# Three cross-attentions with the last key's shares turned beside the inverse sums, and two changes of order in other sublayers

## The reference

```
L1/L2/L3 cross-attention (16 heads of 16 features; 257 keys):
  q = ln(x) Wq + bq;  k = ctx Wk + bk;  v = ctx Wv + bv
  w = softmax(q.k * scale + bias or mask)        # over 257 keys
  x += (w v) Wo + bo
L1 attention (complex, one head): two real parts of q.k summed, softmax over 32 keys, x += out Wo + bo
L0 feed-forward: layer norm twice; 8 fixed experts, 256 rows each:
  xa = ln2 A + b + ln1;  h = gelu(xa W1[e] + b1[e]);  o = h W2[e] + b2[e];  x += gelu(o N + bn)
```

## Time and profile before

| | before |
|---|---|
| median of 3 runs | 3566.3 us (3560.57 to 3572.57) |
| profiled execution | 3571.8 us, its span 3570.0 us |
| mean granted TensorE clock | 0.958 of full |
| busy PE / its weight loads | 3298.9 us (92%) / 2646.9 us (74%) |
| busy DVE / ACT / POOL | 2152.4 (60%) / 1428.5 (40%) / 1017.6 (29%) us |

### The profile page before, as it was taken

How to read it: one execution, slowest core, us unless ns; L and a number is a source line. 1 busy time by engine, 2 the same in 40 slices (tenths; PEclk the granted TensorE clock), 3 DMA queues, 4 the chain that set the end, 5 groups by cost and what they waited for, 6 DMA issues and landing times. The chain is left out here.

```text
span 3570.0 us, 105629 instructions
## 1 busy us (share of the span) xinstructions
PE 3298.9 (92%) x39322; PEld 2646.9 (74%) x39322; DVE 2152.4 (60%) x7124; ACT 1428.5 (40%) x4209; POOL 1017.6 (29%) x1587
## 2 busy tenths in 40 slices
PE   8988889999986999999999999887999999998799
PEld 6767777777765888888877777774666788878576
DVE  3766225555656888889645555763334566558545
ACT  2334335555532333333245555541111455555222
POOL 0112113333342444445333333442110111112421
PEclk9999999999997999999999999978999999999799
DMA  6653334212103000000041111033112411110323
GB/s 208 216 175 154 102 94 108 61 56 56 64 1 140 3 3 3 2 3 2 2 99 43 40 47 46 2 111 124 46 47 72 87 38 38 41 34 2 108 79 114
DMA packets 149258, 238.26 MB, mean 67 GB/s; under 512 B 14456, under 2 KB 121720, under 8 KB 147176
## 3 DMA queue, kind: packets, MB, share of 16 engines
q1 hardware_dynamic: 138816, 203.16, 18.2%
q0 software_dynamic: 10176, 31.47, 3.1%
HBM read 213.61 MB, written 38.94 MB: 71 GB/s over the span
## 5 line engine op out<-in xcount | busy, mean ns | idle before, releaser
L3299 POOL TENSOR_TENSOR l1fu_second_weighed<-l1fu_second,l1fu_parts 128x256 bf16<-128x256 bf16 x384 | 278.7, 753 | 339.2 <-DVE l1fu_second L3540 332.3
L3351 PEld LDWEIGHTS l1fu_ps_u<-l1f_xnT_all,l1f_key_in 128*128 128x128 f32 x2048 | 252.0, 195 | 17.3 <-issue 11.0
L3351 PE MATMUL l1fu_ps_u<-l1f_xnT_all,l1f_key_in 128*128 (+1 forms) x2048 | 254.9, 278 | 8.6 <-issue 5.5
L3362 PE MATMUL l1fu_ps_y<-l1f_key_out,l1fu_units 128*128 128x256 f32 x1024 | 250.6, 389 | 2.0 <-DVE l1fu_units L3548 2.0
L3362 PEld LDWEIGHTS l1fu_ps_y<-l1f_key_out,l1fu_units 128*128 128x128 f32 x1024 | 185.7, 190 | 33.6 <-issue 6.2
L3413 ACT COPY l1fu_plane<-l1fu_ps_p 128x512 f32<-128x512 f32 x128 | 75.1, 586 | 250.4 <-PE l1fu_ps_p L3341 250.4
L3535 DVE TENSOR_TENSOR l1fu_first<-l1fu_index,l1fu_counted 128x1024 bf16<-128x1024 bf16 x128 | 166.8, 1303 | 12.8 <-PE l1fu_ps_p L3341 9.6
L3421 ACT ACTIVATE l1fu_units<-l1fu_ps_u 128x512 f32<-128x512 f32 x128 | 76.6, 598 | 151.9 <-PE l1fu_ps_y L3362 139.9
L1020 ACT ACTIVATE l3x_scores<-l3x_scores,l3x_minus_big 128x257 f32<-128x257 f32 x256 | 129.0, 511 | 2.3 <-DVE l3x_minus_big L1109 2.3
L1020 ACT ACTIVATE l1x_scores<-l1x_scores,l1x_minus_big 128x257 f32<-128x257 f32 x256 | 128.9, 511 | 2.1 <-DVE l1x_minus_big L1109 2.1
L1020 ACT ACTIVATE l2x_scores<-l2x_scores,l2x_minus_big 128x257 f32<-128x257 f32 x256 | 128.8, 511 | 2.1 <-DVE l2x_minus_big L1109 2.1
(11 more groups left out here) (743 smaller groups left out, 8383.6 us busy)
## 6 DMA issues: line engine op xcount, KB each, us to landing
rows_by_expert<-in_zeros_dram SPq DMA_DIRECT2D x1, 17544.0 KB
l0x_ctxT<-in_ctx_T_dram SPq DMA_DIRECT2D x32, 514.0 KB, 5.2
l0x_ctx_rows<-in_ctx_dram SPq DMA_DIRECT2D x64, 256.0 KB, 3.3
l0f_w<-in_L_ffn_w_dram SPq DMA_DIRECT2D x16, 1024.0 KB, 5.2
l1x_ctx_sb<-in_ctx_T_dram SPq DMA_DIRECT2D x64, 256.0 KB, 2.8
l2x_ctx_sb<-in_ctx_T_dram SPq DMA_DIRECT2D x64, 256.0 KB, 2.8
l3x_ctx_sb<-in_ctx_T_dram SPq DMA_DIRECT2D x64, 256.0 KB, 2.8
l1x_mask_raw<-in_mask_int_dram SPq DMA_DIRECT2D x16, 514.0 KB, 3.9
```

Source lines behind the costliest of these rows:

```text
L3299: last = nc.gpsimd.tensor_tensor(second_weighed[:, k % 2, part], second[:, k % 2], parts[:, 1 - par, part, TC * k:TC * k + TC].unsqueeze(2 ...
L3351: last = nc.tensor.matmul(ps_u[:, k % 2, j, :], key_in[:, c, JS * k + j, :], xnT_all[:, c, bass.ts(tile, P)], start=(c == 0), stop=(c == C ...
L3362: last = nc.tensor.matmul(ps_y, units[:, k, j, :], key_out[:, JS * k + j, :], start=(k + j == 0), stop=(k == K - 1 and j == JS - 1))
```

## The change

In cross-attention the last key's share no longer holds its values. POOL spreads the bare probability (`tail_share`) with the table that `share` uses; PE turns it beside `share` into the other half of `ps_share`; ACT copies both in one copy of 256 columns; DVE multiplies it with the last key's values, now kept by feature (`v_last`, a number for each partition), adds the output from PSUM, in two instructions of 64 columns, and then weighs from SBUF. The matmul against the identity is gone. The trip through device memory is gone; instead POOL copies `v_last` once a tile. In complex attention `next_norm` stands after `turn_probs`. In the fixed experts the turning of half 1 stands between the two output halves of the second layer, and ACT keeps it before the expert's output.

```diff
@@ cross_attention: gpsimd
+            def put_tail_values(i, n):
+                after(pool, per_batch["o_with_last"][BT - 1], n - 1)
+                nc.gpsimd.tensor_copy(v_last[:], v_tail[:, :, bass.ds(i * BT, BT)]).then_inc(s["tail_values_put"], 1)
...
-            def shares(i, at, before2):
+            def shares(at, before2):
                 if before2:
-                    pool.wait_ge(per_batch["o_ready"][before2[0]], before2[1])
+                    pool.wait_ge(per_batch["shares_turned"][before2[0]], before2[1])
                 pool.wait_ge(per_batch["exp_ready"][b], n)
                 nc.gpsimd.tensor_tensor(tail_share[:, b % 2], scores[:, b, :, K2].unsqueeze(2).broadcast_to([P, R, 32]),
-                                        tails[:, i, b].rearrange("p (r d) -> p r d", r=R), ALU.mult).then_inc(
-                    per_batch["tail_share_ready"][b], 1)
+                                        core.table("same_half").unsqueeze(1).broadcast_to([P, R, 32]),
+                                        ALU.mult).then_inc(per_batch["tail_share_ready"][b], 1)
...
+                    if not first and t == 0:
+                        put_tail_values(i, n)
                     if ahead:
-                        if first and t == BT - 1:
-                            pool.wait_ge(s["rest_of_tails"], 32)
-                        shares(i + (t + 1) // BT, ahead, before)
+                        shares(ahead, before)
-            def load_tails(name, first, count):
...
@@ tensor
-                for c in range(C):
-                    last = nc.tensor.matmul(ps_vt, ctx_tail[:, c, :], wt["v"][:, c, :],
-                                            start=(c == 0), stop=(c == C - 1))
+                for oc in range(C):
+                    for c in range(C):
+                        last = nc.tensor.matmul(ps_vt[:, oc * B:oc * B + B], wt["v"][:, c, oc * P:oc * P + P],
+                                                ctx_tail[:, c, :], start=(c == 0),
+                                                stop=(c == C - 1 and "bv" not in rows))
+                    if "bv" in rows:
+                        last = nc.tensor.matmul(ps_vt[:, oc * B:oc * B + B], rows["bv"][0:1, oc * P:oc * P + P],
+                                                core.table("ones", 1)[:, 0:B], start=False, stop=True)
...
             def turn_shares(at, before):
                 if before:
-                    pe.wait_ge(per_batch["o_weighed"][before[0]], before[1])
+                    pe.wait_ge(per_batch["o_with_last"][before[0]], before[1])
+                pe.wait_ge(per_batch["tail_share_ready"][b], n)
+                nc.tensor.transpose(ps_share[:, P:2 * P], tail_share[:, b % 2].rearrange("p r d -> p (r d)"), ident)
                 pe.wait_ge(per_batch["share_ready"][b], n)
-                nc.tensor.transpose(ps_share, share[:, b % 2].rearrange("p r d -> p (r d)"), ident).then_inc(
+                nc.tensor.transpose(ps_share[:, 0:P], share[:, b % 2].rearrange("p r d -> p (r d)"), ident).then_inc(
                     per_batch["shares_turned"][b], 1)
...
             def outputs(at):
                 pe.wait_ge(per_batch["shares_kept"][b], n)
-                pe.wait_ge(per_batch["tail_share_ready"][b], n)
-                nc.tensor.matmul(ps_out, tail_share[:, b % 2].rearrange("p r d -> p (r d)"), ident, start=True,
-                                 stop=False, skip_group_check=True)
...
@@ scalar
-                nc.scalar.copy(shareT[:, b % 2], ps_share).then_inc(per_batch["shares_kept"][b], 1)
+                nc.scalar.copy(shareT[:, b % 2].rearrange("p a n -> p (a n)"), ps_share).then_inc(
+                    per_batch["shares_kept"][b], 1)
@@ vector
+                dve.wait_ge(s["tail_values_put"], n)
                 dve.wait_ge(per_batch["o_ready"][b], n)
-                nc.vector.tensor_tensor(weighed[:].rearrange("p c h q -> p (c h q)"), ps_out, shareT[:, b % 2],
+                for c in range(C):
+                    of_chunk = slice(64 * c, 64 * c + 64)
+                    last = nc.vector.scalar_tensor_tensor(lastT[:, of_chunk], shareT[:, b % 2, 1, of_chunk],
+                                                          v_last[:, c, b:b + 1], ps_out[:, of_chunk], ALU.mult,
+                                                          ALU.add)
+                last.then_inc(per_batch["o_with_last"][b], 1)
+                dve.wait_ge(per_batch["o_with_last"][b], n)
+                nc.vector.tensor_tensor(weighed[:].rearrange("p c h q -> p (c h q)"), lastT[:], shareT[:, b % 2, 0],
                                         ALU.mult).then_inc(per_batch["o_weighed"][b], 1)
@@ complex_attention: vector turn
-                if there(i, -1):
-                    next_norm(i - 1, i)
                 if there(i, 3):
                     norm_stats(dve, nc, s, i + 4, core.x[:, i + 3, :], stats[:], mean[:])
                 if there(i, 0):
                     turn_probs(i + 1)
+                if there(i, -1):
+                    next_norm(i - 1, i)
@@ fixed_experts_ffn: tensor turn
                 if now:
-                    second_layer(e + 1)
+                    second_layer(e + 1, 0)
                 if ahead:
                     turn_normed(e + 2, 1)
+                if now:
+                    second_layer(e + 1, 1)
+                if ahead:
                     projection(e + 2)
@@ fixed_experts_ffn: scalar turn
                     keep_turned(e + 2, 0)
+                    keep_turned(e + 2, 1)
                 if now:
                     keep_expert_output(e + 1)
-                if ahead:
-                    keep_turned(e + 2, 1)
-                if now:
```

More of the change, by code:

```diff
@@ L647, in cross_attention @@
                      exp_ready inv_ready share_ready tail_share_ready probs_turned_1 probs_turned_2 probsT_1 probsT_2
-                     shares_turned shares_kept o_ready o_weighed oT_kept""".split()}
+                     shares_turned shares_kept o_ready o_with_last o_weighed oT_kept""".split()}
         pack = core.pack(tag)
@@ L658, in cross_attention @@
         k_tail = sb("k_tail", [P, C, B])
-        v_tail = sb("v_tail", [B, D])
-        tails = sb("tails", [P, NT, BT, P])
+        v_tail, v_last = sb("v_tail", [P, C, B]), sb("v_last", [P, C, BT])
         kT = sb("kT", [P, BT, C, KEYS])
@@ L677, in cross_attention @@
         ps_o, ps_x = ps("ps_o", [P, 512]), ps("ps_x", [P, 512])
-        ps_out, ps_share, ps_kt = ps_o[:, 0:P], ps_o[:, P:2 * P], ps_o[:, 256:256 + C * B]
+        ps_out, ps_share = ps_o[:, 0:P], ps_o[:, P:3 * P]
+        ps_kt, ps_vt = ps_o[:, 256:256 + C * B], ps_p[:].rearrange("p r k -> p (r k)")[:, 0:C * B]
         ps_q, ps_y = ps_x[:, 0:D], ps_x[:, D:2 * D]
-        ps_vt = ps_p[0:B].rearrange("p r k -> p (r k)")[:, 0:D]
         def halves(bank):
@@ L798, in _ @@
             put_tail_keys(0, 1)
+            mask_bias(1)
             pool.wait_ge(s["tail_values"], 1)
-            nc.gpsimd.dma_start(core.tail_values, v_tail[:]).then_inc(s["tail_stored"], 16)
-            mask_bias(1)
-            pool.wait_ge(s["tail_stored"], 16)
-            load_tails("first_tails", 0, 1)
-            load_tails("rest_of_tails", 1, NT - 1)
-            pool.wait_ge(s["first_tails"], 32)
-            shares(0, (0, 1), None)
+            put_tail_values(0, 1)
+            shares((0, 1), None)
             all_tiles(pool, turn)
@@ L918, in outputs @@
                                 ps_out[of_pair, 64 * c:64 * c + 64], v[:, b, kc, c * P + 32 * r:c * P + 32 * r + 32],
-                                probsT[:, b % 2, kc, r, 64 * c:64 * c + 64], start=False, stop=(kc == 1),
+                                probsT[:, b % 2, kc, r, 64 * c:64 * c + 64], start=(kc == 0), stop=(kc == 1),
                                 skip_group_check=True, tile_position=(0, 32 * r))
@@ L1001, in keep_tail_keys, with keep_tail_values @@
                 last.then_inc(s["tail_keys"], 1)
+            def keep_tail_values():
+                act.wait_ge(s["tail_values_ready"], 1)
+                nc.scalar.copy(v_tail[:].rearrange("p c b -> p (c b)"), ps_vt).then_inc(s["tail_values"], 1)
             def keep_keys(at, src=ps_kv):
@@ L1058, in _ @@
             keep_tail_keys()
+            keep_tail_values()
             keep_keys((0, 1), first_keys[0])
@@ L1086, in spread_q @@
                 last.then_inc(s["q_spread"], 1)
-            def keep_tail_values():
-                dve.wait_ge(s["tail_values_ready"], 1)
-                if "bv" in rows:
-                    nc.vector.tensor_tensor(v_tail[:], ps_vt, rows["bv"][0:B], ALU.add).then_inc(s["tail_values"], 1)
-                else:
-                    nc.vector.tensor_copy(v_tail[:], ps_vt).then_inc(s["tail_values"], 1)
             def maxima(at):
@@ L2137, in first_layer, with second_layer @@
                     last.then_inc(h_ready[k], 1)
-            def second_layer(n):
-                pe.wait_ge(s["w2_loaded"], n * 32)
-                after(pe, s["eoT_ready"], n - 1)
```

(18 more changed lines are left out.)

10 lines of the change are left out of this document (2 added, 8 removed).

## The result

Median 3513.1 us (3511.7 to 3519.6, 4 runs) against 3563.4 us (3558.7 to 3572.6, 4 runs) of the kernel before on the same chip: ratio 0.9854, 95% interval 0.9836 to 0.9873, so 50.3 us less. The profiled execution took 3514.2 us, with a span of 3512.3 us; before's took 3571.8 us. The forecast was 3514 us. The total fits; one of its three terms, the cross-attentions, does not, as the tile periods show. The tile period is the distance of two tile outputs (L929 before, L925 after) on PE.

What follows compares the result with a forecast made beforehand. PE's stream bounds the cross-attentions, a DVE and POOL chain l1a, PE's stream with holes l0f. Savings of 30.8 + 7.0 + 15.2 = 53 us from the profiled 3571.8, adjusted to the median, gave 3514 us; 8-in-10 range 3500 to 3533.

Steps and rivals of the forecast that it cites:

- L909's removal, 0.32 us: Cross-attention, PE: without the identity matmul, L917 starts loading when L854's last stream ends, saving 0.32 us a turn.
- Transpose, 0.11 us: Cross-attention, PE: one more transpose beside L902 costs 0.11 us a turn, bounds 0.10 and 0.31.
- Masked tiles, -0.63: l1x and l2x: turn 2 waits on POOL and gains nothing; the three other turns save 0.63 us a tile.
- `weigh`, +0.43: Cross-attention, DVE: added instructions cost 0.43 us, hidden in idle time except in the drain, 0.4 us a sublayer.
- Cross-attentions, 30.8 us: l1x, l2x and l3x together: 30.8 us saved after the drain's cost, bounds 10 and 60.
- l1a, 7.0: Complex attention: moving `next_norm` behind `turn_probs` saves 0.59 us in each of 12 turns, 7.0 us in all.
- l0f, 15.2: Fixed experts: the hole before the projection goes, 2.17 us in each of 7 experts, 15.2 us in all.
- (a): Values' copy reaches PE later, turns 0 and 2 win nothing: 20 us less, 3534; chance 0.11 together with (e).
- (e): DVE's added work reaches PE in turn 1: 18 us less, 3532; chance 0.11 together with (a).
- (b): Cross-attention, PE: L917's loads hide too, 0.21 us more a turn, 19 us more in all, 3495; chance 0.05.
- (c): The added orders meet something in l0f or l1a and give half: 11 us less, 3525; chance 0.07.
- (d): Cross-attentions: PE tips to 1.2 GHz; beyond 13 turns the gain is gone, at 25 turns 3613; chance 0.03.

Runs made afterwards that it cites:

- the second chip: Kernels before and after run again, unchanged, on another chip: before 3511.4 us, after 3464.0 us, ratio 0.9881 against before.
- the two parts alone: Kernel before with only the cross-attention change, 3533.1 us, and kernel before with only the two changes of order, 3529.3 us.
- the masked tile's experiment: Kernel after, with POOL's shares ahead of the next tile's mask bias in turn 1: 3492.8 us, ratio 0.9800 against before.

## Why the prediction was right, and where it was not

**L909's removal, 0.32 us: mis-sized, 0.23.** The step said that L917 "will not load until that stream is through. So L917 starts at 2965.78". The kernel without L909 and after both show 0.22 to 0.23 us. What I dropped is the gap. Before, L869 on a part of the array comes after L902's full-array stream with 0.17 us of idle before it. From L902's load to L869's it is 0.31 us. A transpose follows its like after 0.11 us, so L902's matmul starts about 0.11 us after its load and streams for about 0.11 us; the rest, 0.09 us, is a gap between the end of the stream and the load for a part of the array. By the stream's end at 2965.78 and this gap L917 comes at 2965.87, and 0.23 us are saved. The row that told it I had read, and used only to say that nothing overlaps.

**Transpose, 0.11 us: right.** Shown twice, by the transpose added to before (+0.43 us in four turns) and by after minus the kernel without L909 (0.45). The net is 0.12 us a turn in place of 0.21.

**Masked tiles, -0.63: -0.50.** Three turns at 0.12 are 0.36. The remaining 0.14 came from turn 2, where the step said "That path does not get shorter". It got shorter: from the load of turn 1's scores to the last share's load in turn 2 it is 7.36 us (688.56 - 681.20) where it was 7.50 (711.03 - 703.53, L869's row). POOL's share takes 0.40 us for 0.58. In before it ran beside DVE's spreading of the queries (709.66 to 710.66), in after that is over when it begins (687.87 and 688.11). That one makes the other longer is read from this overlap and not tested by itself. That the bias is this wait's whole cause is shown by the kernel with the bias last (26.53 us).

**`weigh`, +0.43: +0.51.** Hidden in the tiles, as said (DVE's idle time went from 2.07 to 1.39 us). Not hidden in the drain, +0.55 for +0.4. ACT's copy of both shares takes 0.40 us for 0.29, as estimated, and the trip through memory was worth nothing, as said: from l1x's first statistics to its first tile output it is 54.3 us in before and after.

**Cross-attentions, 30.8 us: 18.8 by the tiles.** Within the bounds of 10 to 60, but 12 us short.

**l1a, 7.0: right, 7.5 measured.** PE's 16 tiles span 50.6 us for 58.1. Twelve turns were shortened, as counted, by 0.63 us on average: the forecast took the 4.00 us of one turn for all, and in the middle every other one was 4.20. The section's -7.0 agrees better than it should: its start is 1.1 us longer in after's profile. **l0f, 15.2: right**, 7 x 2.19 = 15.3.

**The total, 53 us: 50.3 measured, some 42 explained by the three parts** (18.8 + 7.5 + 15.3). The rest lies in stretches that the change leaves alone. In the pair of profiles of the second chip the spans differ by 50.0 us: l0f -17.9, l1a -8.0, the three cross-attentions -16.5, together -42.4, and -7.6 elsewhere. A part of this is the granted clock, which I had read in the cross-attentions alone. A mean between 0.5 and 1 is a stretch that ran in part at 1.2 and in part at 2.4 GHz. In l0f, whose steady experts take 18.15 us in both profiles of after, the first expert took 21.75 us in one and 19.06 in the other. The windows, columns as in the earlier trace rows; first after's first profile, then after on the second chip:

```profile
355.30:377.00 21.70, 20.58 (x79) 17.01 (x80) 4.55 (x14) 6.88 (x17) 3.22 (x8) 0.78 0.18 57
```

```profile
357.90:377.00 19.10, 17.97 (x80) 15.34 (x81) 4.55 (x14) 6.91 (x17) 3.22 (x8) 0.92 0.20 64
```

The work is the same to one matmul, PE has nearly the same idle time in both, and the clock is 0.78 and 0.92. The start of l1a, from the first statistics to the first turned rows, is the other case; first before, then the kernel with the two orders alone:

```profile
990.20:1005.90 15.70, 15.66 (x71) 13.53 (x72) 1.88 (x6) 0.59 (x1) 1.57 (x4) 0.67 0.00 1
```

```profile
970.50:981.20 10.70, 10.70 (x71) 9.82 (x72) 1.84 (x6) 0.59 (x1) 1.57 (x4) 1.00 0.01 2
```

PE is busy throughout, and the same matmuls take 5 us less at the full level. The kernel without L909, whose l1a is before's, has the 10.8 us too, so this is not the order of `next_norm`. Some of the 9 us by which the two parts alone gave more than both together can lie in such stretches. In l2a, 3.4 us shorter in the second pair, the clock is 0.955 for 0.912. The stretch from l1f's first normed rows to its first units takes 48.4 to 48.6 us at 0.68 in the two profiles of after and with the cross-attention part alone, and 50.2 to 50.8 us at 0.63 or 0.64 in six of the other seven. Two of those six have the cross-attention part as well, and the kernel without L909 took 51.6 us at 0.67, so the clock is not all of it. No run shows that the change sets the level in any of these stretches; I forecast none of them.

One difference is not the clock. From the first to the last load of l1f's units it is 639.1 to 639.4 us in all five profiles with the new cross-attention and 640.9 to 642.7 in the five without, at 0.99 in all. Nothing in the diff touches them. Its cause stays open; that the program's instructions lie elsewhere is only a guess.

So the right total is in part luck: it owes some 9 us to what I had not forecast. The three parts as measured would have given about 3525 us, 12 us too high. The forecast also set out from 3566.3 us for before, which came down to 3563.4 with a fourth run.

**Rivals.** (a) and (e), a new wait before the keys or the next rows: not there. L841 waits for nothing but its context's loads at the sublayer's start. The values' copy ends 0.17 us before the keys where it ended 0.39 before them; another 0.05 us nearer cost l3x nothing. (b), L917's loads hide too: the 0.33 us of idle before L913 refute it. The Trainium skill, "TensorE: Matmul & The Clock Gate", Part 2, has weight loads pulled ahead where row groups don't conflict or the spare buffer is the target. The trace agrees for full-array loads: L841's first load starts at 2901.02, when the last of L878's four matmuls has only just started (2901.02 to 2901.29). It does not where the load changes to a part of the array. (c), half of the orders' gain: the kernel with the orders alone shows all of it. (d), the clock: 1.00 in the streams of the cross-attentions, with ten transposes in a turn.

## What to carry over

Where a stream changes from the whole array to parts of it, count three things: no overlap, the stream's own end, and a gap (here 0.09 us); read the gap from the nearest such change in the trace. Work that one engine needs for the next tile belongs behind what another engine is waiting for in this one: moving the mask's bias behind the shares gave 18 us, almost as much as the whole cross-attention part. When a sum fits the total, hold each term against its own period as well, read the granted clock of the stretches that you did not touch, and time the kernel before on the same chip: two chips differed here by as much as the change brought.

## What the hardware showed that I had not expected

- Two chips ran the same program, at different times, in 3560.9 and 3511.8 us. The tile periods agree to 0.01 us; 49.7 of the 58.5 us between the two profiles of before are in the two sublayers whose experts' weights are loaded.
- The same 71 matmuls at the start of l1a took 15.7 us at a granted clock of 0.67 and 10.7 us at 1.00, in kernels whose code is the same there.
- DVE's and POOL's instructions take longer where they overlap. POOL's share of 128x128 takes 0.58 us beside DVE's spreading of the queries and 0.40 where that is over. With the bias last, DVE's addition of two halves, 0.23 us elsewhere, takes 0.94 us in turn 1 of the masked tiles, where POOL's bias begins beside it at 683.86 (the row above, in the masked tile's experiment):

```profile
684.07 0.94 DVE L1154 TENSOR_TENSOR l1x_oT<-l1x_weighed 128x64 f32<-128x64 f32 x1
```

- On DVE's queue an instruction that needs the result of the one before starts late. The multiply (0.29 us) starts 0.51 us after the pair that it needs (0.47 us together), and the addition that needs the multiply starts 0.40 us after it (2901.38 to 2901.78). Instructions without such a tie start closer than their lengths: that pair follows an inversion of 0.17 us after 0.10 us (2900.77 to 2900.87).
